# New order for group 0, twelve tiles saved early, earlier mean products and two additions on VectorE

## What is computed

```python
def reference(x, cond_512, W, b):            # x (4, 1024, 512), cond (4, 256), W (1536, 512)
    hidden = concatenate([cond_512, cond_512], axis=-1)
    x_mean = mean(x, axis=1, keepdims=True)
    fused = concatenate([x, x_mean * ones_L, hidden[:, None, :] * ones_L], axis=-1)
    return x + relu(einsum('bld,do->blo', fused, W) + b)
```

## Time and profile before

| | us |
|---|---|
| median of 3 runs | 104.46 (104.31 to 104.62) |
| the profiled execution: its time | 105.41 |
| the profiled execution: its span | 103.3 |
| TensorE busy | 96.9 (94% of the span) |
| VectorE busy | 80.9 (78%) |
| ScalarE busy | 47.3 (46%) |
| GpSimd busy | 41.5 (40%) |

### The profile page before, as it was taken

The page is one execution under the profiler, slowest core; times in us unless marked ns, Lnnn a source line. Parts: engine busy times, 40 slices in busy tenths (PEclk is TensorE's granted clock), DMA queues, the critical chain, the costliest instruction groups (busy, mean ns, idle before and its releaser), DMA issues.

```text
span 103.3 us, 1722 instructions
## 1 busy us (share of the span) xinstructions
PE 96.9 (94%) x523; PEld 78.2 (76%) x523; DVE 80.9 (78%) x146; ACT 47.3 (46%) x116; POOL 41.5 (40%) x37
## 2 busy tenths in 40 slices
PE   5959999999999999999999999999999999999940
PEld 2339999778888786888888886888888868888930
DVE  3173578999899999999999966999999976557630
ACT  3267335795508379497396002973951007310000
POOL 1029700000000003999846501488485089992000
PEclk9999999999999999999999999999999999999999
DMA  2999999999999997999999595000780870595994
GB/s 61 293 300 261 234 233 238 268 274 249 268 296 232 251 226 222 254 244 274 303 331 293 154 229 162 0 0 0 181 226 0 210 196 1 171 290 132 251 309 168
DMA packets 35439, 21.39 MB, mean 207 GB/s; under 512 B 2021, under 2 KB 33129, under 8 KB 35433
## 3 DMA queue, kind: packets, MB, share of 16 engines
q1 hardware_dynamic: 33848, 20.13, 78.9%
q10 hardware_dynamic: 1584, 1.18, 4.3%
HBM read 12.91 MB, written 8.39 MB: 206 GB/s over the span
## 4 chain that ended last, share of the span: by engine, by line
PE 89%; ACTq 4%; ACT 2%; issue 0%; DVE 0%
PE ps_y L459 76%; PE ps_y L560 4%; PE ps_y L562 4%; PE ps_y L561 4%; ACTq L168 2%; ACTq L158 2%; PE ps_mean L478 1%; PE ps_const L527 1%; ACT xh L259 1%; ACT w1h L252 1%; ACT L244 0%; DVE w L449 0%; PE ps_y L583 0%; ACT act_warm L244 0%
## 5 line engine op out<-in xcount | busy, mean ns | idle before, releaser
L234 POOL TENSOR_TENSOR xa<-xa,back 128x512 f32 x28 | 36.1, 1314 | 45.1 <-DVE back L346 45.1
L459 PE MATMUL ps_y<-xh,w1h 128*128 (+2 forms) x128 | 43.9, 370 | 1.1 <-ACT w1h L252 1.1
L459 PE MATMUL ps_y<-xl,w1h 128*128 (+2 forms) x128 | 43.0, 363 | 0.0
L459 PE MATMUL ps_y<-xh,w1l 128*128 (+2 forms) x128 | 42.9, 363 | 0.0
L259 ACT ACTIVATE xh<-ps_xt 128x512 fp32r<-128x512 f32 (+1 forms) x36 | 19.8, 550 | 19.4 <-DVE ps_xt L333 19.4
L459 PEld LDWEIGHTS ps_y<-xh,w1h 128*128 128x128 f32 x128 | 22.6, 188 | 6.7 <-ACT xh L259 1.6
L339 DVE TENSOR_TENSOR xl<-ps_xt,xh 128x512 fp32r<-128x512 f32 (+1 forms) x36 | 22.2, 618 | 4.7 <-ACT xh L259 4.7
L333 DVE STREAM_TRANSPOSE ps_xt<-xa 128x512 f32<-128x512 f32 (+1 forms) x36 | 22.3, 642 | 4.5 <-DMA xa<-in_x_dram 4.2
L459 PEld LDWEIGHTS ps_y<-xh,w1l 128*128 128x128 f32 x128 | 22.6, 189 | 3.8
L459 PEld LDWEIGHTS ps_y<-xl,w1h 128*128 128x128 f32 x128 | 22.7, 189 | 3.5
L277 ACT ACTIVATE relu_t<-ps_y,bias 128x512 f32<-128x512 f32 x20 | 13.5, 686 | 16.7 <-DVE bias L380 15.3
(11 more groups left out here) (34 smaller groups left out, 34.1 us busy)
## 6 DMA issues: line engine op xcount, KB each, us to landing
xa<-in_x_dram SPq DMA_DIRECT2D x60, 128.0 KB, 4.3
out_dram<-xa SPq DMA_DIRECT2D x28, 256.0 KB, 4.1
w<-in_L_cond_W_dram SPq DMA_DIRECT2D x4, 256.0 KB, 6.2
w<-in_L_cond_W_dram SPq DMA_DIRECT2D x2, 512.0 KB, 6.9
w<-in_x_dram SPq DMA_DIRECT2D x4, 256.0 KB, 3.9
out_dram<-w SPq DMA_DIRECT2D x3, 256.0 KB, 3.3
...
```

The lines of the kernel that those rows point to most:

```text
L234: nc.gpsimd.tensor_tensor(rows, rows, back[:, t], ALU.add).then_inc(added, 1)
L459: return nc.tensor.matmul(ps_y[:, t, ls], lhs, rhs, start=start, stop=stop, skip_group_check=True)
```

## The change

**Group 0.** Halves are kept for k = 0 and 1 only. The order is: half 0, k = 0 and 1 with w1h (xh, xl), then both with w1l; half 1, k = 0 and 1; then k = 2 and 3 over all 512 rows, k = 3 tile by tile. The low and high halves of w1h[0] are written by ScalarE (tiles 0, 1) and VectorE (tiles 2, 3). The second half of x of group 0 is loaded ahead of w1's pieces 2-3, which are now all on SyncE's queue. The condition's loads go behind group 1's.

**Group 1** computes its tiles 0 and 1 interleaved over k.

**Saves.** SAVED is 12: group 2 is copied out as well. The tiles of group 0 go into w1's own place once w1l is made (place(n)), the others into relu_t. save(11) stands between relu(3) and relu(4). A new count y_free covers saves (n < 12) and relus (n from 12 on); TensorE waits for it in place of y_saved and relu_done.

**Pieces of groups 4 to 7.** VectorE prepares them at n = 2 to 17 (X_TURNS); ScalarE after relu(6) to relu(13) and relu(16) to relu(23) (X_ROUNDS).

**Bias.** w2x has two buffers and the mean products alternate between ps_mean and ps_const. mean_terms(1) comes ahead of const_row and of sum_bias(0). mean_bias(0) moves one tile later, with const_product; mean_bias(1) to group 2, t = 3, k = 1; mean_bias(2) to group 4, t = 3, k = 1; mean_bias(3) to group 6, t = 2, k = 2 (half a tile earlier). The last bias is stored by one DMA of four rows and loaded by another, both on ScalarE's queue around relu(24) and relu(26).

**Additions.** VectorE adds x to tiles 26 and 27 (late_added); GpSimd has 26 left. TensorE's and GpSimd's loops over groups are written out.

```diff
+    DVE_ADDS = 2
+    SAVED = 3 * NK
+    X_TURNS = range(2, 2 + NK * (G - SLOTS))
+    MEANS_AT = ((2 * H, 3, 1), (3 * H, 2, 2))
+    X_ROUNDS = (*range(6, 6 + 2 * NK), *range(4 * NK, 6 * NK))
...
+        def place(n):
+            return w1[:, n] if n < NK else relu_t[:, (n - NK) % RELU_RING]
...
-            load_w1(sp, 2, NK, LOW)
             load_x0(sp, 1, LOW)
+            load_w1(sp, 2, NK, ORDER)
+            load_x(sp, 1, ORDER)
...
-            load_w1(act, 2, NK, HIGH)
             load_x0(act, 1, HIGH)
...
             x_high(0)
+            w1_high(0)
             x_high(1)
-            w1_high(0)
             w1_high(1)
-            for k in range(2, NK):
-                x_high(k)
-                w1_high(k)
+            for n in range(2, NK + 2):
+                x_high(n)
+            w1_high(2)
+            x_high(NK + 2)
+            w1_high(3)
+            x_high(NK + 3)
+            n_x = pieces_to(1)
+            for k in range(NK):
+                x_high(n_x + k)
+                save(k)
...
             for n in range(len(tiles)):
+                if n == NK:
+                    save(2 * NK + 3)
+                if n == NK * (LAST - 1):
+                    store_bias(act)
+                elif n == NK * (LAST - 1) + 2:
+                    spread_bias(act)
                 relu(n)
-                for _n in range(steps_of_x(n, 2)):
+                if n in X_ROUNDS:
                     x_high(n_x)
                     n_x += 1
...
+                if n >= len(tiles) - DVE_ADDS:
+                    g, t = tiles[n]
+                    rows = xa[:, g, :, Q * t:Q * t + Q]
+                    dve.wait_ge(turned_back, n + 1)
+                    nc.vector.tensor_tensor(rows, rows, back[:, t], ALU.add).then_inc(late_added, 1)
-                for _n in range(steps_of_x(n, 3)):
-                    if n % NK == 0:
+                if n in X_TURNS:
+                    k = X_TURNS.index(n) % NK
+                    if k == 0:
                         turn_x(n_x)
...
+            pe.wait_ge(y_free, 2)
+            for k in range(NK):
+                pe.wait_ge(xl_ready, pieces_to(1) + k + 1)
+                for t in (0, 1):
+                    last = product(1, k, t)
+                    if k == NK - 1:
+                        last.then_inc(y_ready, 1)
...
-            with pe.Fori(1, B - 1) as b:
+            for g in range(H + 1, LAST):
                 for t in range(NK):
-                    pe.wait_ge(relu_done, NK * H * b + t + 1)
...
+                    pe.wait_ge(y_free, NK * (g - 1) + t + 1)
+                    for k in range(NK):
+                        if t == 0:
+                            pe.wait_ge(xl_ready, pieces_to(g) + k + 1)
+                        elif (g, t, k) in MEANS_AT:
+                            mean_bias(g // H)
+                        last = product(g % SLOTS, k, t)
```

More of the change, by code:

```diff
@@ L84, in build @@
     bias_line = nc.dram_tensor("bias_line", [D], F32).ap()
+    DVE_T = NK // 2
     def by_tile(rows):
@@ L410, in _ @@
             turn_and_split(n_x, n_x + NK)
+            mean_terms(1)
             dve.wait_ge(const_summed, 1)
@@ L506, in _ @@
[L506 to L517 removed]
+                    group0(k, ls, w1h, xh, start=(half == 0 and k == 0))
@@ new lines, in _ @@
+                    pe.wait_ge(xl_ready, NK * half + k + 1)
+                    group0(k, ls, w1h, xl)
+                    if half == 1:
+                        group0(k, ls, w1l, xh)
+                if half == 0:
+                    for k in range(NK // 2):
+                        pe.wait_ge(w1l_ready, k + 1)
+                        group0(k, ls, w1l, xh)
+            for k in range(NK // 2, NK):
+                pe.wait_ge(w1h_ready, k + 1)
+                pe.wait_ge(xl_ready, NK + k + 1)
+                if k < NK - 1:
+                    group0(k, slice(0, NL), w1h, xh)
+                    group0(k, slice(0, NL), w1h, xl)
+                    pe.wait_ge(w1l_ready, k + 1)
+                    group0(k, slice(0, NL), w1l, xh)
+                else:
+                    pe.wait_ge(w1l_ready, k + 1)
+                    for t in range(NK):
+                        product(0, k, t).then_inc(y_ready, 1)
```

183 lines of the change are left out of this document (90 added, 93 removed).

## The result

The changed kernel takes **108.4 us** (median of 4 runs, 108.1 to 109.06); the kernel before took 104.54 beside it (104.31 to 104.93). The ratio is 1.037, 95% interval 1.032 to 1.043: 3.9 us slower. Forecast were 106.0 and at most 107.3. The sign was right, the size was not. The profiled execution has a span of 107.3 us and a time of 109.06, the slowest of the four; before, 103.3 and 105.41.

What follows compares the result with a forecast made beforehand. TensorE's run of matmuls was taken as the bound. The start's -0.25, group 4's wait of +1.77 and 0 for the tail made +1.5 us, from a median of 104.46 to 106.0; range 105.1 to 107.3, 8 in 10.

Steps and rivals of the forecast that it cites:

- steps on the landing of half 1 and on k = 1: Group 0: TensorE waits 0.6 us at k = 1, then 0.6 us for half 1, landing at 9.7.
- the -0.25 of the sum: Groups 0 and 1 together: group 2 begins at 30.05 in place of 30.30, 0.25 us earlier.
- Its 0.49 us: Group 1: time lost at matmuls waiting for low parts, some 0.49 us, to go with tiles 0 and 1 interleaved.
- Group 4's wait: Before group 4's first matmul: TensorE waits 1.66 us for relu(12), plus 0.11 for the restart, 1.77 us lost.
- S: Start of group 3's matmuls, from which the count to relu(12)'s end, 12.40 us later, was made.
- that rival: Clock falls to 1.2 GHz in the wait before group 4: 108.7 us; chance 0.04, shared with the tail.
- The argument against the rival: End of the kernel before: TensorE idle for the last 4.0 us at granted clock 1.00, so no fall expected.
- the step that failed: End of the kernel: the tail of 4 us stays, 0 added, up to 0.5 us more if stores run together.
- GpSimd's eight last additions: Last groups: they take 10.56 us and end at 93.5; two fewer are 2.6 us less.
- mean_bias(2) was asked only: Before relu(16): TensorE has 2.1 us of matmuls behind it, the bias steps and relu take 1.8; no wait.
- The row with 0.99 us: VectorE's bsum at 57.31, ending with GpSimd's addition; each moved addition may be held up by up to 1.3 us.

Runs made afterwards that it cites:

- e8: The kernel before with one part alone: VectorE adds x to tiles 26 and 27, GpSimd has 26 left; 103.25 us, ratio 0.989.
- e7: The changed kernel with the loads and group 0 of the kernel before, group 1 still interleaved; 109.26 us, ratio 1.044.
- e2: The changed kernel with all five stores of group 7 issued from ScalarE's queue; 109.26 us, ratio 1.044.
- e11: Against e6: turn_back(20) and (21) ahead of mean_terms(3), last mean product at tile 3, k = 0; 105.0 us, ratio 1.005.
- e6: The changed kernel with ScalarE's pieces behind relu(6)-(9) and relu(12)-(15), VectorE's pieces of groups 6 and 7 at n = 12 to 19; 104.83 us, ratio 1.003.

## Why the prediction came out as it did

**The start (steps on the landing of half 1 and on k = 1).** Right in kind. The first matmul came at 6.48, forecast 6.5. k = 1 began at 7.91, forecast 8.21, after an idle time of 0.24 us, forecast 0.6, because w1's second part landed 0.3 us earlier in this execution. Half 1 was used from 10.30 on, forecast 9.7, bounds 8.96 and 11.29. In the nine profiled executions with this start TensorE's wait before half 1 was under 0.1 us three times and at most 1.27 us, in the very execution shown above; the mean is 0.42, forecast 0.6. The start of const_product, 30 matmuls into group 2, was at 35.98 to 37.55 there, 36.72 in the mean; the three executions with the old start stand at 36.44 to 37.20, moved to the same matmul, 36.71 in the mean. So the -0.25 of the sum came out near 0.

**Group 1.** Its 0.49 us went, as forecast. But they were no fixed loss of the old order: e8 has the old start and no such wait (group 2 came 10.9 us after group 1). I took one execution's landing of group 1's x for a property of the program.

**Group 4's wait.** Right. From the end of group 3 (54.46) S is 43.58, and relu(12) was to end at S + 12.40 = 55.98; it ended at 55.99. TensorE lost 1.58 + 0.11 us, forecast 1.66 + 0.11, and putting the order back brought 1.8 (0.9 where the tail had been mended first).

**The clock.** The granted clock stayed at 1.00 through this wait and to 106.5 us, so that rival is out, although its 108.7 lies nearer to the measured 108.4 than the forecast does. The falls in waits in mid kernel that the Trainium skill describes (TensorE: Matmul & The Clock Gate, "HAM oscillation — how this bites in real kernels") were not seen in any wait of 1.4 us here. The argument against the rival, 4.0 us idle without a fall, was weaker than it looked. In e8 the last matmul ends near 98.45, and the granted clock falls to 0.50 (1.2 GHz) 2.0 us later:

```profile
98.40:100.40 2.00, 0.05 (x1) 0.00 (x0) 0.43 (x1) 0.00 (x0) 0.00 (x0) 1.00 0.80 291
100.50:101.20 0.70, 0.00 (x0) 0.00 (x0) 0.00 (x0) 0.00 (x0) 0.00 (x0) 0.50 0.00 0
```

**The tail: the step that failed.** "With everything 1.5 us later, group 6 is stored some 6 us before the last matmul ends ... I take 0; up to 0.5 us more." Measured is +1.95 us in the profile, and group 6 is released at 96.66, 4.3 us before the last matmul begins (100.99), not 6. Three things in that step were wrong.
1. The tail of the kernel before was taken as a fixed 4 us. It was a backlog of the DMA engines, as e8 shows, where it is 2.7 us.
2. "GpSimd's eight last additions ... two fewer are 2.6 us less" took the row's tiles as given. The order of VectorE's rows shows that two more tiles, (18) and (19), had moved behind the pause; the run is as long as before. The difference in order on VectorE was read only at its start, where group 4's pieces begin, not at its end, where the same table (X_TURNS) ends two tiles earlier.
3. mean_bias(2) was asked only whether TensorE or the bank of relu(16) waits for it. TensorE doesn't. But relu(16) opens the row of pieces of groups 6 and 7, at whose end stand mean_terms(3) and the last turns. GpSimd's last run begins 20.1 us behind the third bias row in all thirteen kernels that leave mean_terms(3) in its place.

The account closes by rows. Group 4 starts 56.04 - 54.11 = 1.93 us later: the 1.58 of the wait, and 0.35 by which this execution was late already. The bias row comes 9.56 - 8.74 = 0.82 later behind that: the mean product stands three matmuls further back (0.68), behind the restart (0.11). Two more tiles in front of group 5's end make 7.56 - 5.07 = 2.5. Together 5.2: group 5's stores are issued from 93.26 on, before from 88.03. From there to the end of the span it is 14.0 us, was 15.2, as VectorE's additions close the gap (1.2). 5.2 - 1.2 = 4.0, which is the difference of the spans.

That the span ends nearly the same time after group 5's first store holds in all kernels with VectorE's additions and group 7's stores on SyncE's queue: 13.7 to 14.5 us in all twelve, from 87.28 and 101.2 (e8) to 93.80 and 107.9 (e7). With all additions on GpSimd it is 15.2 and 15.7; with group 7's stores on ScalarE's queue (e2) it is 15.5. I had looked for the bound on TensorE alone, and at this point it was not TensorE's.

**The additions.** The row with 0.99 us was the right one: they took 0.94 and 1.05 us in the changed kernel, and 1.20 and 1.04 in e8, against 0.71 for one of them in e11, so they were held up. The Trainium skill's rule (SBUF — State Buffer, "Who interferes with whom") agrees in kind. By it alone the edit looked worthless; the runs show 1.2 to 1.9 us of gain, since here it counts when group 6 is complete.

**What stays open.** e6 holds VectorE's additions and is no faster than the kernel before, while e8 is 1.6 us faster than e6. The rows say where it arises. Both have group 4's first matmul at the same time (53.38 and 53.35), but e6's third bias row comes at 63.58, e8's at 62.10, and group 5's first store at 88.71 against 87.28. In e6 the third w2x is ready 2.0 us later (62.4 against 60.4), and turn_back(10) and (11) stand between it and the bias row; in e8 they stand ahead of both. No run tries that apart. Nor was it tried why half 1 lands up to 1.3 us earlier or later from run to run.
